# Scaling the second pair of probabilities on ScalarE in the last four steps of a decoder layer

## The chip, the cores and the metric

One core of one Trainium2 chip. The time is device microseconds of one execution of the program; the median of 3 runs before the change is 962.37 us (961.47 to 962.55). Engines are called as in the profile: PE is TensorE, DVE is VectorE, ACT is ScalarE, POOL is GpSimd, SP is SyncE, which issues the DMAs.

## The reference

A decoder layer in float32: x (8 rows of 128 tokens, 512 features) goes through a causal self-attention, then a cross-attention, then a linear layer with 4-bit weights, each with a layer norm in front and a residual behind. The cross-attention, where the change lies, has 8 key heads with 4 query heads each, head size 128, and 256 keys (128 of the context, 128 of the row itself):

```
q, k = rms_norm(latents @ Wq), rms_norm(kv @ Wk);  v = kv @ Wv
probs = softmax(q @ k.T / sqrt(128))     # 32 heads, 128 x 256 each
x = x + (probs @ v) @ Wo
x = x + layernorm(x) @ dequantized_weights.T + bias
```

## The kernel before

The program is two parts, one after the other: self-attention, then `cross_attention_and_linear`. The second part runs 64 steps, s = 8 j + b, for key head j and row b. Each step treats the 4 query heads of one key head for one row. Every float32 operand of a matrix product is split into a high and a low part (`_hi`, `_lo`), and a product is three matmuls. The high part is a Copy on ACT, the low part a subtraction on DVE or POOL.

The order of each engine is written out by hand, and semaphores join the engines. For a step s the work goes like this:

- PE makes scores(s) into two PSUM banks, `ps_s[0]` for heads 0 and 1, `ps_s[1]` for heads 2 and 3. It then does the values of step s-2, the keys and values of s+3, the queries of s+3 and the output projection of s-2.
- DVE takes the row maxima of each bank (`biases`, L1220), ACT the exponentials with their sums (`exps`, L1120), in place in PSUM.
- `probs(s, h)` on DVE (L1227 to L1236) takes for each pair h of heads the reciprocals of the sums (`inv`), multiplies the bank by them into `p` (L1232), and writes the 32x32-block transposes into `p_blocks` (L1236).
- SP stores `p_blocks` to `p_scratch` and loads it back in transposed order into `pT_raw`; one step later ACT makes its high part (`probs_high`, L1143) and POOL its low part (`probs_low`, L1039).
- The keys and queries of the next step come back from memory in the same way; ACT makes their high parts (`queries_keys_high`, L1147 and L1149), DVE the keys' low part (`keys_low`, L1259), POOL the queries' low part (`queries_low`, L1032).
- The output of step s-2 is split by ACT (`output_high`, L1154) and DVE (`output_low`, L1270), projected by PE and added to x by DVE (`residual`, L1266).

In the last round (j = 7, `LAST`) the rows become final one by one, and the linear layer begins between the steps: POOL prepares its weights (`linear_weights`, L1052) and, per row, `row_rstd` and `row_and_bias` (L1068, tile `base`, named `raw_wq` in the trace since it lies in that buffer). DVE takes `statistics`, `normalised` (L1305) and the finished row (`out_row`, L1320), ACT `xn_high` (L1165), DVE `xn_low_row` (L1310), PE the transposes and `linear`.

What matters here is the order on three engines in the last four steps (b = 4 to 7, s = 60 to 63):

- ACT: `exps(s, 0)`, then for b >= 5 `output_high(s-2)` and `exps(s, 1)`, for b = 4 the other way round; `queries_keys_high(s+1)` (not in s = 63); `linear_high(1)` in s = 60; `xn_high(b-4)`; in s = 60 `keys_values(63)`; `probs_high(s-1)`.
- POOL: `row_rstd(b-3)`, ..., `queries_low(s+1)`, `probs_low(s-1)`, and then `linear_weights(4)` (s = 60) or `row_and_bias(b-5)`.
- DVE: `biases(s)`, `normalised(b-4)`, `probs(s, 0)`, then `output_low(s-2)` and `probs(s, 1)` (b = 4: the other way round), `keys_low(s+1)`, `xn_low_row(b-4)`, ..., `residual(s-2)`, `statistics(b-2)`, and `out_row(b-5)`, which stands ahead of the next step's `biases`.

Of the kernel before, what the change touches and what calls it, by code (L numbers as in the profile page):

```python
# [17 lines left out]
ACT = mybir.ActivationFunctionType  # L18
# [13 lines left out]
KV = 2 * S  # L32
# [5 lines left out]
def wait(eng, sem, count):  # L38

    if not (isinstance(count, int) and count <= 0):  # L40
        eng.wait_ge(sem, count)
# [788 lines left out]
def cross_attention_and_linear(nc, mem, io):  # L830
# [7 lines left out]
    with ExitStack() as ctx:  # L838
# [12 lines left out]
        NKV, STEPS, R = 2 * XD, XKVH * B, 32  # L851
        LAST = XKVH - 1
# [15 lines left out]
        total, inv = sb("total", [P, XG]), sb("inv", [P, XG])  # L868
        p = sb("p", [P, XG, KV])
        p_blocks = sb("p_blocks", [P, 8, XG, R])  # L870
# [5 lines left out]
        packed, scale = raw_wq[:, 0:2, :].bitcast(I32), raw_wq[:, 2:4, :]  # L876
# [233 lines left out]
        @block.scalar  # L1110
        def _(act):
            def weights_high(w, raw, landed, count, hi):
                act.wait_ge(landed, 16 * count)
                act.activation(w[0][:], raw[:], ACT.Copy).then_inc(hi, 1)

            def exps(s, h):
                act.wait_ge(bias_ok, 2 * s + h + 1)
                for g in range(2 * h, 2 * h + 2):
                    scores = ps_s[g // 2][:, g % 2 * KV:(g % 2 + 1) * KV]
                    e = act.activation(scores, scores, ACT.Exp, bias=bias[:, g:g + 1],  # L1120
                                       scale=q_rms[:, s % 4, g:g + 1], accum_out=total[:, g:g + 1])
                e.then_inc(exp_done, 1)

            def keys_values(s):

                act.wait_ge(kv_ps, s + 1)
                for t in range(2):
                    i = act.activation(k_squares[:, t, :], kv_rows[:, t, 0:XD], ACT.Square, scale=XD ** -0.5,
                                       accum_out=k_mean[:, t:t + 1])
                i.then_inc(k_mean_ok, 1)  # L1130
                act.activation(v[s % 5][0][:], kv_rows[:, :, XD:], ACT.Copy).then_inc(v_hi, 1)

            def query_sums(s):
                act.wait_ge(q_blocked, s + 1)
                wait(act, q_ms, s)
                for g in range(XG):
                    i = act.activation(q_squares[:, g, :], ps_q[:, g * XD:(g + 1) * XD], ACT.Square, scale=XD ** -0.5,  # L1137
                                       accum_out=q_mean[:, g:g + 1])
                i.then_inc(q_mean_ok, 1)

            def probs_high(s):
                act.wait_ge(p_loaded[s % 4], landed(s))
                act.activation(pT_hi_sb[:], f32(pT_raw[s % 2][:]), ACT.Copy).then_inc(pT_hi, 1)  # L1143

            def queries_keys_high(s):
                act.wait_ge(qk_loaded[s % 4], landed(s))
                act.activation(kT[0][:].rearrange("p (i t c) -> p i t c", i=4, t=2), qk_raw[s % 2][:, :, XG:, :], ACT.Copy,  # L1147
                               scale=key_scale[:, 0:1]).then_inc(kT_hi, 1)
                act.activation(qT[0][:].rearrange("p g (i c) -> p g i c", i=4),  # L1149
                               qk_raw[s % 2][:, :, 0:XG, :].rearrange("p i g c -> p g i c"), ACT.Copy).then_inc(qT_hi, 1)  # L1150

            def output_high(s):
                act.wait_ge(o_ps, s + 1)
                act.activation(oT[0][:].rearrange("p g (i c) -> p g i c", i=4),  # L1154
                               ps_o[:].rearrange("p (i g c) -> p g i c", i=4, g=XG), ACT.Copy).then_inc(o_hi, 1)

            def linear_high(h):
                act.wait_ge(weights_ok, h + 1)
                act.activation(w[0][:, 2 * h:2 * h + 2, :], weights[h], ACT.Copy).then_inc(w_hi, 1)

            def xn_high(b):
                act.wait_ge(xnT_ps, b + 1)
                if b >= 2:
                    act.wait_ge(f_ps, b - 1)
                act.activation(xnT[b % 2][0], ps_xn[:].rearrange("p (c s) -> p c s", c=C), ACT.Copy).then_inc(xn_hi, 1)  # L1165

            keys_values(0)
            query_sums(0)
            keys_values(1)
            query_sums(1)  # L1170
            queries_keys_high(0)
            keys_values(2)
            query_sums(2)
            for s in range(STEPS):
                j, b = divmod(s, B)
                if j < LAST and b == 0:
                    weights_high(wkv[(j + 1) % 2], raw_wkv, wkv_in, j + 1, wkv_hi)
                if b == 2:
                    wait(act, y_ps, B * j)
                    weights_high(wo, raw_wo, wo_in, j + 1, wo_hi)  # L1180
                if j < LAST and b == 3:
                    weights_high(wq[(j + 1) % 2], raw_wq, wq_in, j + 1, wq_hi)
                exps(s, 0)
                if j == LAST and b >= 5:
                    output_high(s - 2)
                    exps(s, 1)
                else:
                    exps(s, 1)
                    if s >= 2:
                        output_high(s - 2)  # L1190
                if s + 1 < STEPS:
                    queries_keys_high(s + 1)
                if j == LAST:
                    if b in (2, 4):
                        linear_high(b // 2 - 1)
                    if b >= 4:
                        xn_high(b - 4)
                if s + 3 < STEPS:
                    keys_values(s + 3)
                if s:  # L1200
                    probs_high(s - 1)
                if s + 3 < STEPS:
                    query_sums(s + 3)
            output_high(STEPS - 2)
            xn_high(4)
            probs_high(STEPS - 1)
            output_high(STEPS - 1)
            xn_high(5)
            xn_high(6)
            xn_high(7)  # L1210

        @block.vector
        def _(dve):
# [10 lines left out]
                        i = dve.tensor_scalar(bias[:, g:g + 1], neg_max[:, g:g + 1], q_rms[:, s % 4, g:g + 1], None, ALU.mult)  # L1224
                    i.then_inc(bias_ok, 1)

            def probs(s, h):  # L1227
                two = slice(2 * h, 2 * h + 2)
                dve.wait_ge(exp_done, 2 * s + h + 1)
                dve.reciprocal(inv[:, two], total[:, two]).then_inc(inv_ok, 1)  # L1230
                dve.wait_ge(inv_ok, 2 * s + h + 1)
                dve.tensor_tensor(p[:, two, :], ps_s[h][:].rearrange("p (g k) -> p g k", g=2),  # L1232
                                  inv[:, two].unsqueeze(2).broadcast_to([P, 2, KV]), ALU.mult).then_inc(p_ok, 1)
                wait(dve, p_stored, 16 * s)
                dve.wait_ge(p_ok, 2 * s + h + 1)
                dve.transpose(p_blocks[:, :, two, :], p[:, two, :].rearrange("p g (m r) -> p m g r", r=R)).then_inc(p_blocked, 1)  # L1236
# [20 lines left out]
            def keys_low(s):  # L1257
                dve.wait_ge(kT_hi, s + 1)
                dve.scalar_tensor_tensor(kT[1][:].rearrange("p (i t c) -> p i t c", i=4, t=2), qk_raw[s % 2][:, :, XG:, :],  # L1259
                                         key_scale[:, 0:1], f32(kT[0][:]).rearrange("p (i t c) -> p i t c", i=4, t=2),  # L1260
                                         ALU.mult, ALU.subtract).then_inc(kT_lo, 1)
# [66 lines left out]
            for s in range(STEPS):  # L1328
                j, b = divmod(s, B)
                biases(s)  # L1330
                if j == LAST:
                    linear_bits(b)
                    if b >= 4:
                        normalised(b - 4)
                probs(s, 0)
                if j == LAST and b >= 5:
                    output_low(s - 2)
                    probs(s, 1)
                else:
                    probs(s, 1)  # L1340
                    if s >= 2:
                        output_low(s - 2)
                if s + 1 < STEPS:
                    keys_low(s + 1)
                if j == LAST and b >= 4:
                    xn_low_row(b - 4)
                if s + 3 < STEPS:
                    values_low(s + 3)
                    queries_blocked(s + 3)
                    keys_blocked(s + 3)  # L1350
                if s >= 2:
                    residual(s - 2)
                if j == LAST:
                    if b >= 2:
                        statistics(b - 2)
                    if b >= 5:
                        out_row(b - 5)
# [219 lines left out]
```

## Time and profile before

| | |
|---|---|
| median of 3 runs | 962.37 us (961.47 to 962.55) |
| profiled execution, its own time | 963.0 us |
| its span, first to last instruction | 961.2 us |
| PE busy | 920.2 us (96%) |
| DVE busy | 727.1 us (76%) |
| ACT busy | 607.3 us (63%) |
| POOL busy | 561.3 us (58%) |
| mean granted TensorE clock | 0.989 |

A busy share is over the whole span. The last four steps and the tail behind them lie from 888 us on. The start of a step is best seen in the first `neg_max` instruction (L1220) of the step on DVE: 888.89, 900.35, 912.10 and 922.96 us for s = 60 to 63.

### The profile page before, as it was taken

The page shows a single profiled execution, that of the slowest core. Times are in us where ns is not written, and L with a number is a line of the kernel's source. Part 1 is how long each engine was busy: PE and PEld are TensorE (multiplying, and loading weights), DVE is VectorE, ACT ScalarE, POOL GpSimd, SP SyncE. Part 2 cuts the span into 40 slices and gives each one's busy share as a digit, 9 for nine tenths or more (in the row PEclk, how much of TensorE's full clock was granted, in tenths as well). Part 3 has the DMA queues.
Part 4 walks back from the last instruction along what each step waited for, and adds up shares of the span by engine and source line. Part 5 has one row for each costly group of instructions (what it writes and reads, how often), then busy time and mean ns, then how long its engine had stood idle before and what let it go on. Part 6 is the DMA issues. An engine that isn't in the chain of part 4 may idle for free.

```text
span 961.2 us, 17529 instructions
## 1 busy us (share of the span) xinstructions
PE 920.2 (96%) x5488; PEld 792.0 (82%) x5496; DVE 727.1 (76%) x1556; ACT 607.3 (63%) x2229; POOL 561.3 (58%) x591
## 2 busy tenths in 40 slices
PE   6899998888999999999999999999999999999987
PEld 5677776677888888888888888888888888888776
DVE  6788888638777777777777777777777777788985
ACT  4688888537656766575666666656766676565541
POOL 6332233338845865686558557855765686558742
PEclk9899999989999999999999999999999999999999
DMA  5000020037665566566656655765566556654431
GB/s 209 12 13 12 13 88 13 1 115 268 223 218 168 175 199 203 173 189 210 214 163 198 213 168 173 228 213 173 168 213 197 165 172 208 209 173 149 156 124 56
DMA packets 101164, 149.84 MB, mean 156 GB/s; under 512 B 11856, under 2 KB 77392, under 8 KB 98896
## 3 DMA queue, kind: packets, MB, share of 16 engines
q1 hardware_dynamic: 101072, 148.71, 48.6%
q8 instruction: 45, 0.74, 0.3%
q14 instruction: 47, 0.39, 0.1%
HBM read 87.85 MB, written 60.82 MB: 155 GB/s over the span
## 4 chain that ended last, share of the span: by engine, by line
PE 72%; DVE 4%; ACT 2%; POOL 2%; issue 1%; DVEq 0%; POOLq 0%
PE ps_kv L73 18%; PE ps_q L73 17%; PE ps_y L73 17%; PE ps_s L73 9%; PE ps_o L73 9%; ACT ps_s L1120 1%; POOL pT_raw L1039 1%; PE ps_f L73 1%; DVE neg_max L1220 0%; DVE p L1232 0%; DVE p_blocks L1236 0%; DVE kT_lo L1259 0%; DVE f_stats L1295 0%; DVE x L1266 0%; POOL qT_lo L1032 0%
## 5 line engine op out<-in xcount | busy, mean ns | idle before, releaser
L1120 ACT ACTIVATE ps_s<-ps_s,bias,q_rms 128x256 f32<-128x256 f32 x256 | 136.7, 535 | 139.8 <-DVE bias L1224 139.8
L1032 POOL TENSOR_TENSOR qT_lo<-qk_raw,qT_hi 128x512 fp32r<-128x512 f32 x64 | 84.5, 1320 | 202.9 <-ACT qT_hi L1149 202.9
L1039 POOL TENSOR_TENSOR pT_raw<-pT_raw,pT_hi_sb 128x1024 fp32r<-128x1024 f32 x63 | 151.7, 2409 | 5.8 <-ACT pT_hi_sb L1143 5.5
L1137 ACT ACTIVATE q_squares<-ps_q 128x128 bf16<-128x128 f32 x256 | 67.2, 277 | 112.5 <-DVE qk_blocks L1254 112.5
L73 PE MATMUL ps_y<-wo_hi,oT_hi 128*128 128x512 f32 x252 | 100.0, 397 | 4.0 <-DVE oT_lo L1270 4.0
L73 PE MATMUL ps_q<-wq_lo,xT_hi 128*128 128x512 f32 x256 | 101.5, 397 | 0.0
L1236 DVE STREAM_TRANSPOSE p_blocks<-p 128x512 f32<-128x512 f32 x128 | 91.1, 712 | 13.3
L73 PE MATMUL ps_q<-wq_hi,xT_hi 128*128 128x512 f32 x256 | 101.1, 395 | 0.0
L73 PE MATMUL ps_q<-wq_hi,xT_lo 128*128 128x512 f32 x256 | 101.1, 395 | 0.0
L73 PE MATMUL ps_y<-wo_lo,oT_hi 128*128 128x512 f32 x252 | 99.5, 395 | 0.0
L73 PE MATMUL ps_y<-wo_hi,oT_lo 128*128 128x512 f32 x252 | 99.4, 394 | 0.0
L1266 DVE TENSOR_TENSOR x<-ps_y,x 128x512 f32<-128x512 f32 x64 | 44.2, 691 | 68.2 <-PE ps_y L73 67.3
L1232 DVE TENSOR_TENSOR p<-ps_s,inv 128x512 f32<-128x512 f32 x128 | 88.5, 691 | 4.4
L1220 DVE TENSOR_REDUCE neg_max<-ps_s 128x2 f32<-128x512 f32 x128 | 87.7, 686 | 5.3
L1254 DVE STREAM_TRANSPOSE qk_blocks<-ps_q 128x512 f32<-128x512 f32 x64 | 45.8, 715 | 42.7 <-PE ps_q L73 42.6
L73 PE MATMUL ps_kv<-wkv_hi,cT_hi 128*128 128x256 f32 x256 | 73.1, 285 | 4.1 <-DVE k_sb L1244 4.1
L73 PE MATMUL ps_s<-kT_hi,qT_hi 128*128 128x256 f32 x256 | 72.6, 284 | 2.7 <-DVE kT_lo L1259 1.3
L73 PE MATMUL ps_kv<-wkv_hi,xT_hi 128*128 128x256 f32 x256 | 72.9, 285 | 0.0
L73 PE MATMUL ps_kv<-wkv_hi,cT_lo 128*128 128x256 f32 x256 | 72.7, 284 | 0.0
L73 PE MATMUL ps_kv<-wkv_hi,xT_lo 128*128 128x256 f32 x256 | 72.6, 284 | 0.0
L73 PE MATMUL ps_kv<-wkv_lo,xT_hi 128*128 128x256 f32 x256 | 72.6, 284 | 0.0
L73 PE MATMUL ps_kv<-wkv_lo,cT_hi 128*128 128x256 f32 x256 | 72.6, 284 | 0.0
(233 smaller groups left out, 2913.3 us busy)
## 6 DMA issues: line engine op xcount, KB each, us to landing
p_scratch<-p_blocks SPq DMA_DIRECT2D x64, 512.0 KB, 3.0
pT_raw<-p_scratch SPq DMA_DIRECT2D x256, 128.0 KB, 3.0
qk_scratch<-qk_blocks SPq DMA_DIRECT2D x64, 384.0 KB, 3.5
qk_raw<-qk_scratch SPq DMA_DIRECT2D x256, 96.0 KB, 3.0
raw_wq<-in_x_wq SPq DMA_DIRECT2D x8, 1024.0 KB, 7.7
raw_wo<-in_x_wo SPq DMA_DIRECT2D x8, 1024.0 KB, 8.2
raw_wkv<-in_x_wkv SPq DMA_DIRECT2D x8, 512.0 KB, 5.0
ctx_raw<-in_ctxT SPq DMA_DIRECT2D x8, 256.0 KB, 2.6
```

Of the source, the lines that this page charges most:

```text
L73: mm = pe.matmul(out, lhsT, rhs, start=start and i == 0, stop=stop and i == len(terms) - 1)
L1032: pool.tensor_tensor(qT[1][:].rearrange("p g (i c) -> p g i c", i=4), qk_raw[s % 2][:, :, 0:XG, :].rearrange("p i g c -> p g i c"), f32(qT ...
L1039: pool.tensor_tensor(raw, f32(raw), f32(pT_hi_sb[:].rearrange("p i t x -> p (i t x)")), ALU.subtract).then_inc(pT_lo, 1)
L1120: e = act.activation(scores, scores, ACT.Exp, bias=bias[:, g:g + 1], scale=q_rms[:, s % 4, g:g + 1], accum_out=total[:, g:g + 1])
L1137: i = act.activation(q_squares[:, g, :], ps_q[:, g * XD:(g + 1) * XD], ACT.Square, scale=XD ** -0.5, accum_out=q_mean[:, g:g + 1])
L1220: dve.tensor_reduce(neg_max[:, two], ps_s[h][:].rearrange("p (g k) -> p g k", g=2), AX.X, ALU.max, negate=True).then_inc(max_ok, 1)
L1232: dve.tensor_tensor(p[:, two, :], ps_s[h][:].rearrange("p (g k) -> p g k", g=2), inv[:, two].unsqueeze(2).broadcast_to([P, 2, KV]), ALU.mu ...
L1236: dve.transpose(p_blocks[:, :, two, :], p[:, two, :].rearrange("p g (m r) -> p m g r", r=R)).then_inc(p_blocked, 1)
L1254: dve.transpose(qk_blocks[:, :, 0:XG, :].rearrange("p j x c -> p x j c"), ps_q[:].rearrange("p (g j r) -> p g j r", g=XG, r=R)).then_inc(q ...
L1266: dve.tensor_tensor(acc[:, b, :], ps_y[:], acc[:, b, :], ALU.add).then_inc(acc_ok, 1)
```

## The change

In steps 60 to 63 DVE no longer multiplies the second pair of heads. DVE takes only the reciprocals of the sums (`inverse_totals`), and ACT makes two Copies of 128x256 with the reciprocal as scale (`second_probs`), one for each head, behind the next step's `queries_keys_high` and ahead of `xn_high` and `probs_high`. The block transposes of the second pair stay on DVE, but behind `output_low` and `keys_low`. On ACT `output_high(s-2)` now stands ahead of `exps(s, 1)` in s = 60 too.

```
+            def second_probs(s):
+                act.wait_ge(inv_ok, 2 * s + 2)
+                for g in (2, 3):
+                    i = act.activation(p[:, g, :], ps_s[1][:, g % 2 * KV:(g % 2 + 1) * KV], ACT.Copy, scale=inv[:, g:g + 1])
+                i.then_inc(p_ok, 1)
...
                 exps(s, 0)
-                if j == LAST and b >= 5:
+                if j == LAST and b >= 4:
                     output_high(s - 2)
                     exps(s, 1)
+                    if s + 1 < STEPS:
+                        queries_keys_high(s + 1)
+                    second_probs(s)
...
-            def probs(s, h):
+            def inverse_totals(s, h):
                 two = slice(2 * h, 2 * h + 2)
                 dve.wait_ge(exp_done, 2 * s + h + 1)
                 dve.reciprocal(inv[:, two], total[:, two]).then_inc(inv_ok, 1)
+
+            def second_probs_blocked(s):
+                wait(dve, p_stored, 16 * s)
+                dve.wait_ge(p_ok, 2 * s + 2)
+                dve.transpose(p_blocks[:, :, 2:, :], p[:, 2:, :].rearrange("p g (m r) -> p m g r", r=R)).then_inc(p_blocked, 1)
...
                 probs(s, 0)
-                if j == LAST and b >= 5:
+                if j == LAST and b >= 4:
+                    inverse_totals(s, 1)
                     output_low(s - 2)
-                    probs(s, 1)
+                    if s + 1 < STEPS:
+                        keys_low(s + 1)
+                    second_probs_blocked(s)
...
-                if s + 1 < STEPS:
+                if s + 1 < STEPS and not (j == LAST and b >= 4):
                     keys_low(s + 1)
```

## Rows read from the trace of the kernel before

**Rows 1.** Chain that ended last, step 60 to tail: start us, us, what.
```profile
895.96 2.81 PE ps_y L73 x12
...
907.01 2.41 DVE kT_lo L1259
...
917.37 0.96 ACT pT_hi_sb L1143
...
918.39 2.61 POOL pT_raw L1039
...
921.00 1.26 POOL raw_wq L1068
...
930.79 1.66 PE ps_o L73 x6
...
945.04 0.95 PE ps_y L84 x4
```

**Rows 2.** Timeline of ACT, steps 60 to 63: start us, length us, instruction.
```profile
895.47 0.42 ACT L1131 ACTIVATE v_hi<-ps_kv 128x256 fp32r<-128x256 f32 x1
...
895.73 1.10 ACT L1143 ACTIVATE pT_hi_sb<-pT_raw 128x1024 fp32r<-128x1024 f32 x1
...
904.08 0.53 ACT L1147 ACTIVATE kT_hi<-qk_raw,key_scale 128x256 fp32r<-128x256 f32 x1
...
904.48 0.65 ACT L1149 ACTIVATE qT_hi<-qk_raw 128x512 fp32r<-128x512 f32 x1
...
905.13 0.60 ACT L1165 ACTIVATE wkv_hi<-ps_xn 128x512 fp32r<-128x512 f32 x1
...
926.70 0.61 ACT L1165 ACTIVATE wkv_hi<-ps_xn 128x512 fp32r<-128x512 f32 x1
```

**Rows 3.** Timeline of POOL, steps 60 to 63; brackets: idle before, releaser.
```profile
896.91 2.40 POOL L1039 TENSOR_TENSOR pT_raw<-pT_raw,pT_hi_sb 128x1024 fp32r<-128x1024 f32 x1
...
900.53 2.40 POOL L1052 TENSOR_TENSOR wq_lo<-raw_wq,wq_hi 128x1024 fp32r<-128x1024 f32 x1
...
905.21 1.29 POOL L1032 TENSOR_TENSOR qT_lo<-qk_raw,qT_hi 128x512 fp32r<-128x512 f32 x1 [1.26 <-ACT qT_hi L1149]
...
906.76 2.38 POOL L1039 TENSOR_TENSOR pT_raw<-pT_raw,pT_hi_sb 128x1024 fp32r<-128x1024 f32 x1 [0.26 <-ACT pT_hi_sb L1143]
...
909.10 1.48 POOL L1068 TENSOR_TENSOR raw_wq<-x,f_bias 128x512 f32<-128x512 f32 x1
...
928.33 2.40 POOL L1039 TENSOR_TENSOR pT_raw<-pT_raw,pT_hi_sb 128x1024 fp32r<-128x1024 f32 x1 [5.25 <-ACT pT_hi_sb L1143]
```

**Rows 4.** Timeline of DVE, steps 61 to 63; brackets: idle before, releaser.
```profile
902.28 0.93 DVE L1305 TENSOR_SCALAR raw_wkv<-x,f_moments,f_rstd 128x512 f32<-128x512 f32 x1
...
905.33 0.14 DVE L1230 RECIPROCAL inv<-total 128x2 f32<-128x2 f32 x1
...
906.94 2.48 DVE L1259 SCALAR_TENSOR_TENSOR kT_lo<-qk_raw,key_scale,kT_hi 128x256 fp32r<-128x256 f32 x1
...
909.95 0.67 DVE L1266 TENSOR_TENSOR x<-ps_y,x 128x512 f32<-128x512 f32 x1
...
911.49 0.69 DVE L1320 TENSOR_TENSOR raw_wq<-ps_f,raw_wq 128x512 f32<-128x512 f32 x1
...
912.10 0.68 DVE L1220 TENSOR_REDUCE neg_max<-ps_s 128x2 f32<-128x512 f32 x1
...
922.35 0.69 DVE L1320 TENSOR_TENSOR raw_wq<-ps_q,raw_wq 128x512 f32<-128x512 f32 x1 [0.80 <-POOL raw_wq L1068]
...
926.33 0.71 DVE L1236 STREAM_TRANSPOSE p_blocks<-p 128x512 f32<-128x512 f32 x1
...
926.97 0.65 DVE L1270 TENSOR_TENSOR oT_lo<-ps_o,oT_hi 128x512 fp32r<-128x512 f32 x1
```

**Rows 5.** Timeline of PE, step 61: output projection of step 59.
```profile
905.46 0.50 PE L73 MATMUL ps_y<-wo_hi,oT_hi 128*128 128x512 f32 x1 [0.36 <-DVE oT_lo L1270]
```

**Rows 6.** Timeline of SP's DMA issues, step 60: query and key loads.
```profile
895.45 2.22 SPq L941 DMA_DIRECT2D qk_raw<-qk_scratch  x4
```

More of the change, by code:

```diff
@@ L1230, in probs @@
                 dve.reciprocal(inv[:, two], total[:, two]).then_inc(inv_ok, 1)
+            def second_probs_blocked(s):
+                wait(dve, p_stored, 16 * s)
+                dve.wait_ge(p_ok, 2 * s + 2)
+                dve.transpose(p_blocks[:, :, 2:, :], p[:, 2:, :].rearrange("p g (m r) -> p m g r", r=R)).then_inc(p_blocked, 1)
+            def probs(s, h):
+                two = slice(2 * h, 2 * h + 2)
+                inverse_totals(s, h)
                 dve.wait_ge(inv_ok, 2 * s + h + 1)
@@ L1342, in _ @@
                         output_low(s - 2)
-                if s + 1 < STEPS:
+                if s + 1 < STEPS and not (j == LAST and b >= 4):
                     keys_low(s + 1)
```

## The prediction, made before the changed kernel ran

> **What bounds the kernel now.** The page first: over the whole span PE is busy 96%, so in the 60 steps that the change leaves alone PE sets the pace. The last four steps are another regime, so I read them by the chain that ended last. The reader is to see that it leaves PE after the output projection of step 60 [rows 1], passes through DVE's low part of the keys in step 61 (2.41 us of its 2.48), and in step 62 through ACT's high part of the probabilities (917.37), POOL's low part (918.39) and POOL's base row (921.00). In step 63 it takes the same way and comes back to PE at 930.79, with the values of step 62. From there to 945.99 it is PE piece on piece. So the multiplication on DVE that the change takes away lies on no late stretch of this chain, while ACT, which gets the new work, does. Three timelines give the slack. DVE's out row of step 62 sat idle 0.80 us until POOL's base row at 922.35 [rows 4]. POOL's last low part of a full step sat idle 5.25 us for ACT's high part [rows 3] and ended at 930.73; the values on PE started 0.06 us later. On the stretch ACT, POOL, base row, out row there is no slack in step 62, and on ACT, POOL, values none in step 63.
>
> **The change part by part.** The price that the trace doesn't show is c, the time by which one of ACT's new Copies (128x256, PSUM to SBUF, scale from a tile) puts off the next instruction. The nearest rows [rows 2]: `v_hi`, PSUM to SBUF with a constant scale, puts the next off by 0.26 (895.47 to 895.73); `kT_hi`, with a scale from a tile but out of SBUF, by 0.40 (904.08 to 904.48); and if nothing overlapped, its whole 0.53. Reading PSUM is cheaper than SBUF by some 0.05 (a 512-wide Copy lasts 0.60 at 905.13 and 0.65 at 904.48), so I take c = 0.40 - 0.04 = 0.36, with 0.26 and 0.53 as ends. Two Copies are 0.72 us a step.
>
> The Trainium skill, "ScalarE: Activation LUTs", section "What ACT_TABLE_LOAD costs", gives an ACTIVATE as 186 ns plus 0.833 ns per element, 93 ns more for each operand taken from a tile, and 93 ns of overlap: an estimate of 0.40 for c, so 0.3 us more on the sum below. The same page, section "Rules for kernel authors", puts multiplications on VectorE rather than ScalarE, which speaks against this change; no row here shows the product on ScalarE.
>
> *Step 60.* ACT's Copies stand ahead of the linear layer's weights, `xn_high`, the keys of step 63 and `probs_high(59)`; `output_high(58)` only trades places with `exps(60, 1)`. The high part of step 59 moves from 895.73 to 896.45, POOL's low part from 896.91 to 897.6, since it began 0.08 after it [rows 2, 3]. What follows on POOL is nearly back to back, so the linear weights' low part moves by 0.67, from 900.53 to 901.2, and ends at 903.6 and no longer at 902.93. DVE's `normalised(1)`, issued at 902.28, ended at 903.21, 0.28 after that POOL instruction [rows 4]; `kT_lo` in step 61 shows the same, 909.42 against POOL's 909.14 [rows 3, 4]. Such a DVE instruction beside POOL ends 0.28 after it. So it now ends at 903.88, and all behind it on DVE is +0.67. The late transposes (+0.9 us) put off SP's store of the probabilities and, queued behind it, the loads of step 62's queries and keys, from 895.45 to 896.4 [rows 6]. With 2.2 us of issue and 3.0 to land (the page) they land at 901.6 and are wanted at 904.08 [rows 2]: nothing. Term: +0.67 at the front of step 61.
>
> *Step 61.* DVE loses the product and takes the output's low part behind a reciprocal that now stands ahead of it (0.14 long, at 905.33, with its gap 0.17 [rows 4]). The projection's start goes from 905.46 [rows 5] to 906.3. `keys_low` comes at 906.2, while POOL's `qT_lo` runs (905.21 to 906.50 [rows 3]), so by the 0.28 above it ends at 906.8, not at 909.42: the 2.48 us stall is gone. The scores of step 62 are then held by the projection (906.3 + 2.81, the length of one in rows 1), and the residual, at 909.95 [rows 4], comes at 909.3; from it to the out row it was 1.54 us, which gives 910.8 instead of 911.49. But what is late next is POOL's base row. ACT's Copies wait for the reciprocal, now at 905.42 to 905.56, and run from 905.6; queued behind the wait are `xn_high` (905.13 before, 906.3 now) and `probs_high`, 0.5 later. It puts POOL's low part from 906.76 to about 907.95, the base row from 909.10 to 910.3, and its end, at 1.29 us (it lasted 1.48 beside `kT_lo`; POOL's other 512-wide instruction lasts 1.29 [rows 3]), to 911.6. The out row starts at 911.65, 0.16 later than before. So the gain of 2.6 us on `kT_lo` is spent: +0.67 comes in, +0.15 goes out. The first maximum of step 62 moves from 912.10 to 912.25 [rows 4].
>
> *Step 62.* ACT's queue is exponentials, output, exponentials, keys, queries, Copies, `xn_high`, `probs_high`. The reciprocal is early enough; +0.72 on the high part that stands on the chain at 917.37. POOL's low part lasted 2.61 beside `kT_lo` against 2.38 in step 61; now `kT_lo` is done before it, so 0.2 comes back. Base row, out row and the maxima of step 63 follow: +0.5. DVE waits for the Copies with its transposes some 0.4 us; behind it stand `xn_low_row` and the residual, which are due later than the base row lets them go.
>
> *Step 63.* No keys and queries here to cover the reciprocal. It stands behind the first pair's transposes, which hold DVE from 926.33 to 926.97 [rows 4], and ends at about 927.12; `xn_high`, at 926.70 before [rows 2], now waits for it 0.45 us and for the Copies 0.72. That is +1.17 for `probs_high(62)`, POOL's low part and the values at 930.79. DVE's last transposes come 0.15 later in the step than before; the store and load of step 63's probabilities are wanted only after the values, linear(3), a transpose and a projection on PE, which have themselves moved by more: nothing.
>
> *Tail.* From 930.79 to 945.99 nothing on the chain waits [rows 1], so what reaches the values reaches the end.
>
> Sum: 0.15 + 0.5 + 1.17 = +1.8 us. The profiled execution took 963.0 us (span 961.2, and 1.8 around it); its sum is 964.8. It lay 0.6 above the median, so for a median I say 962.4 + 1.8 = **964.2 us**. Each 0.01 us in c counts eight times (two Copies, four steps): at c = 0.26 the sum is +1.0 (963.4), at 0.53 it is +3.2 (965.6).
>
> **The rivals.**
>
> *Dear Copies.* If a Copy puts the next off by 0.47 or more, towards its whole length, the sum is +2.7 to +3.2: about 965.3. For it: DVE reads PSUM at the same time, and no row shows a Copy of just this kind. Against it: both neighbouring rows overlap.
>
> *The early keys' low part carries (the other side).* The place is the end of step 61. By the times above the out row starts at 910.9 + 2c there, if the base row holds it, and at 910.8 if that does not. Against 911.49 the place gains from c = 0.29 down, up to 0.7 us. If the Copies also fill time in which ACT would have stood idle, so that steps 62 and 63 add nothing, the whole gains: 962.4 - 0.7 = 961.7. For it: ACT stands idle for long stretches here, `v_hi`'s 0.26 is under that point, and the stall of 2.48 is the largest single thing in these steps. Against it: ACT's idle time lies behind `probs_high`, not ahead of it, and what POOL waited for in step 63 was ACT [rows 3].
>
> *The linear weights do not pass it on.* If step 60's +0.67 does not reach step 61 (POOL catches up, or `normalised(1)` gets in before the weights), the base row of step 61 ends at 910.9 and the sum is 1.8 - 0.67 = +1.1: 963.5. Against it: POOL's row at 900.53 runs across 902.28 even when it starts 0.67 later.
>
> **How the numbers follow.** My forecast (c between 0.26 and 0.46, all terms) has 0.66, its own range 963.4 to 965.0. Dear Copies 0.13, no passing on 0.13, the other side 0.08. The range reaches from 962.6, between the other side and no passing on, to 965.6, the dear end. About 0.2% (1.9 us) is what a measurement of this kernel can tell from no change. Slower by more means above 964.3: all of dear Copies and somewhat under half of my forecast, 0.13 + 0.29 = 0.42. Faster by more means below 960.4, which even the other side's 961.7 does not reach unless step 62 gains too: 0.04. The rest, 0.54, is within 0.2%.
>
> **What would show it.** Right: a Copy at 0.36 to the next start; the linear weights' low part ending about 903.6 and `normalised(1)` 0.28 after it; `kT_lo` of step 61 under 1 us and starting near 906.2; the out rows of steps 61 and 62 both waiting for POOL's base row; first maxima at about 912.25 and 923.6 for steps 62 and 63; the values of step 62 at 932.6, and from there the same tail. Wrong: an out row that waits for PE or for nothing, POOL's low parts not moving with the Copies, or a tail that shrinks.

## The result, and the profile after

The changed kernel takes 964.87 us (median of 15 runs, 962.79 to 967.47) against 962.63 us before (15 runs): ratio 1.0025, 95% interval 1.0016 to 1.0035, so slower by 1.5 to 3.4 us. The forecast was 964.2 us, slower by 1.8.

The profiled execution of the changed kernel took 963.52 us, and its span is 961.4 us, hardly more than 961.2 before. That is no contradiction: single executions differ by some us in their first part (the last section), and here the first row maximum of step 60 comes at 887.28 us against 888.89. What the change touches begins there. So I measure from that instruction to the start of the last out row; the rows of the changed kernel on DVE:

```profile
887.28 0.67 DVE L1229 TENSOR_REDUCE neg_max<-ps_s 128x2 f32<-128x512 f32 x1
...
898.74 0.67 DVE L1229 TENSOR_REDUCE neg_max<-ps_s 128x2 f32<-128x512 f32 x1
...
910.74 0.68 DVE L1229 TENSOR_REDUCE neg_max<-ps_s 128x2 f32<-128x512 f32 x1
...
922.11 0.68 DVE L1229 TENSOR_REDUCE neg_max<-ps_s 128x2 f32<-128x512 f32 x1
...
958.21 0.69 DVE L1338 TENSOR_TENSOR raw_wq<-ps_q,raw_wq 128x512 f32<-128x512 f32 x1 [1.78 <-PE ps_q L84]
```

The stretch is 70.93 us; before it was 958.04 - 888.89 = 69.15. So +1.78 us, beside a forecast of +1.8. The stretch does not hold all of the difference of the medians, 2.24 us. An execution's own time is longer than its span by 1.72 to 1.85 us in all executions of the kernel before whose span is on record, and by 2.08 to 2.17 in all 15 of the changed kernel (and in the two other kernels below that have the change in all four steps). These 0.35 us lie outside the first and last instruction, and no run shows where they come from. In the table each column is the time since the first row maximum of step 60: the first maximum of steps 61, 62 and 63, the first matmul of the values of step 62, and the start of the last out row.

| kernel | step 61 | step 62 | step 63 | values 62 | last out row |
|---|---|---|---|---|---|
| before | 11.46 | 23.21 | 34.07 | 41.90 | 69.15 |
| changed | 11.46 | 23.46 | 34.83 | 43.78 | 70.93 |
| difference | 0 | +0.25 | +0.76 | +1.88 | +1.78 |

Where it went is in the chain that ended last (columns: start us, us, what), which answers to [rows 1]:

```profile
906.38 2.40 POOL pT_raw L1039
908.77 1.27 POOL raw_wq L1068
...
915.40 0.85 ACT p L1160 x2
916.25 0.49 ACT wkv_hi L1171
916.74 0.96 ACT pT_hi_sb L1143
917.70 0.07 issue
917.76 2.39 POOL pT_raw L1039
920.15 1.25 POOL raw_wq L1068
...
926.65 0.47 ACT p L1160
927.12 0.49 ACT wkv_hi L1171
927.61 0.96 ACT pT_hi_sb L1143
928.57 0.07 issue
928.63 2.38 POOL pT_raw L1039
931.01 0.04 issue
931.06 1.65 PE ps_o L73 x6
```

The stalled `kT_lo` that stood on the chain before is gone from it. ACT's two new Copies (`p`, L1160) are on it instead, in steps 62 and 63, each time with `xn_high`, `probs_high`, POOL's low part and its base row (or PE's values) behind them. In step 61 the chain now runs through POOL, whose low part at 906.38 sat idle 1.51 us for ACT's high part; that part stood behind the Copies at 904.02 (both rows are in the section on the prediction).

### The profile page after: what moved, and what is told of

The parts are those of the page before. It is cut to its first block, busy times and chain, and to the rows that moved or that the text cites. A ratio compares the mean times of both kernels' runs of the same rounds, so it can differ in the third digit from the quotient of the medians.

```text
span 961.4 us, 17533 instructions
## 1 busy us (share of the span) xinstructions
PE 918.6 (96%) x5488; PEld 791.2 (82%) x5496; DVE 723.4 (75%) x1552; ACT 610.9 (64%) x2237; POOL 559.8 (58%) x591
## 4 chain that ended last, share of the span: by engine, by line
PE 71%; DVE 3%; POOL 2%; ACT 2%; issue 1%; DVEq 0%; POOLq 0%
PE ps_kv L73 18%; PE ps_y L73 17%; PE ps_q L73 17%; PE ps_o L73 9%; PE ps_s L73 9%; POOL pT_raw L1039 1%; ACT ps_s L1120 1%; PE ps_f L73 1%; DVE neg_max L1229 0%; POOL qT_lo L1032 0%; DVE p L1250 0%; DVE p_blocks L1254 0%; POOL raw_wq L1068 0%; DVE raw_wq L1303 0%; ACT q_squares L1137 0%
## 5 line engine op out<-in xcount | busy, mean ns | idle before, releaser
L1254 DVE STREAM_TRANSPOSE p_blocks<-p 128x512 f32<-128x512 f32 x124 | 88.2, 711 | 12.9
L1250 DVE TENSOR_TENSOR p<-ps_s,inv 128x512 f32<-128x512 f32 x124 | 85.7, 691 | 4.2
```

## The experiments

Each is read by the stretch above, in one profiled execution of each kernel, since a few tenths of a us are lost in the spread of whole executions. Ten of them were also timed over several executions, and for these a ratio to the kernel before is given; step 60 alone and step 63 alone ran once.

The stretch ends at the start of the last out row, so it leaves out the last store. At the very end SP waits for that store (columns: us in total, times, longest), in the kernel before and in step 61 alone:

```profile
SPq L1007 <- DMA out<-raw_wq: 1.7, 1, 1.7
...
SPq L1007 <- DMA out<-raw_wq: 2.8, 1, 2.8
```

The wait is 2.8 to 2.9 us in all five kernels below that make the change in one step only, and 1.7 us in all others, the changed kernel included. Why is not shown. So in those five some 1.1 us come on top of what the stretch says; their ratios contain them.

**The change in step 61 alone** (step 60, 62 and 63 as before).

```
-                if j == LAST and b >= 4:          # changed kernel, on ACT and on DVE
+                if j == LAST and b == 5:
...
+                elif j == LAST and b >= 5:        # the order of the kernel before
```

> The change in step 61 alone; steps 60, 62 and 63 as before. I measure the stretch from the first row maximum of step 60 to the start of the last out row in the profile: 69.15 us before, 70.93 with the whole change. My theory: each step's two Copies (0.72 us) cost only where they stand ahead of work that POOL and PE wait for, and step 61 alone also removes the 2.4 us stall of the keys' low part. Without step 60's delay the base row of step 61 then ends about 0.5 us earlier than before, so the stretch is 68.5 to 68.8 (-0.35 to -0.65) and the kernel is slightly faster. Rival, the Copies cost their 0.72 us in every step whatever else moves, so each step is worth a quarter of the whole: +0.45, 69.6.

Measured: 68.75 us (-0.40); step 62 begins at 22.85, 0.36 earlier. Ratio 1.0005 (0.9990 to 1.0019). So the Copies do not cost their 0.72 us wherever they are made: in this step the stretch gains. The kernel as a whole does not. From step 60's first row maximum to the end of the span it takes 73.08 us against 72.31 before, because of the last store.

**The change in steps 61 to 63.**

```
-                if j == LAST and b >= 4:
+                if j == LAST and b >= 5:
```

> The change in steps 61 to 63, step 60 as before. My theory: step 60 costs 0.6 to 0.7 us through ACT's queue, POOL's low part of the linear weights and the row normalisation on VectorE that ends with it; so the stretch from step 60's first row maximum to the last out row is 70.1 to 70.35 (whole change 70.93, before 69.15). Rival, step 60's delay is hidden by the base row on POOL that holds step 61 anyway: 70.8 to 71.0, no change from the whole.

Measured: step 62 at 22.83, 0.63 ahead of the whole change; the stretch is 70.56, not 70.1 to 70.35. Ratio 1.0016 (1.0000 to 1.0031). Step 62 lasted 11.57 us against 11.37 in the whole change, and in it the granted clock fell (columns: window, its length, busy time of PE, PEld, DVE, ACT and POOL, clock, DMA share, GB/s):

```profile
910.00:915.00 5.00, 4.95 (x24) 3.85 (x23) 4.00 (x12) 1.77 (x6) 2.21 (x4) 1.00 0.82 240
915.00:920.00 5.00, 3.50 (x12) 2.65 (x11) 3.44 (x7) 4.09 (x10) 2.22 (x2) 0.72 0.16 63
```

Up to step 62 the theory holds, and the end is 0.2 outside its numbers. The slower clock accounts for that. From the start of PE's output projection to the residual that waits for it on DVE the changed kernel took 3.10 us (915.52 to 918.62), this one 4.65:

```profile
916.92 0.58 PE L73 MATMUL ps_y<-wo_hi,oT_hi 128*128 128x512 f32 x1 [1.50 <-DVE oT_lo L1291]
...
921.50 1.30 POOL L1068 TENSOR_TENSOR raw_wq<-x,f_bias 128x512 f32<-128x512 f32 x1
...
921.57 0.69 DVE L1287 TENSOR_TENSOR x<-ps_y,x 128x512 f32<-128x512 f32 x1 [2.52 <-PE ps_y L73]
...
923.12 0.67 DVE L1341 TENSOR_TENSOR raw_wq<-ps_q,raw_wq 128x512 f32<-128x512 f32 x1
```

So the out row came 0.32 us after the end of POOL's base row, which it follows by 0.09 to 0.11 us in the changed kernel: an estimate of 0.2 us for the clock.

**Step 60 alone** (the first experiment's edit with another step).

```
-                if j == LAST and b >= 4:
+                if j == LAST and b == 4:
```

> The change in step 60 alone, steps 61 to 63 as before; one look, read by the stretch from step 60's first row maximum to the last out row (69.15 us before, 70.93 with the whole change). My theory: the two Copies reach the end through GpSimd's low part of the linear weights, beside which the row normalisation of step 61 ends: step 61 starts as before, step 62 0.6 to 0.75 later, and the stretch is 69.7 to 69.9. Rival, PE sets step 60's end and the base row hides the rest: 69.1 to 69.3.

Measured: step 61 at 11.47, step 62 at 23.94 (+0.73), the stretch 69.88 (+0.73). POOL's low part of the linear weights and DVE's normalisation beside it, of this kernel:

```profile
899.12 2.39 POOL L1052 TENSOR_TENSOR wq_lo<-raw_wq,wq_hi 128x1024 fp32r<-128x1024 f32 x1
```

```profile
900.15 1.64 DVE L1326 TENSOR_SCALAR raw_wkv<-x,f_moments,f_rstd 128x512 f32<-128x512 f32 x1
```

The normalisation ends at 901.79, 0.28 after POOL, and lasts 1.64 instead of 0.93 [rows 4].

**Step 63 alone.**

```
-                if j == LAST and b >= 4:
+                if j == LAST and b == 7:
```

> The change in step 63 alone; one look, read by the same stretch. My theory: 0.4 us of waiting for the reciprocal behind the first pair's transposes and 0.72 for the two Copies stand ahead of the last high part that GpSimd and then the values on PE wait for: the values of step 62 start 1.05 to 1.2 later than before against step 60's first row maximum (41.90), and the stretch is 70.1 to 70.4. Rival, a part of it is taken back by the shorter work of VectorE or in PE's tail: 69.2 to 69.8.

Measured: the values of step 62 at 43.06 (+1.16), the stretch 70.21 (+1.06). By the table and these runs, alone or in the whole, the steps are worth +0.73, -0.4, +0.5 and +1.1.

**Copies made twice.**

```
                 for g in (2, 3):
+                    act.activation(q_squares[:, 2 * g - 4:2 * g - 2, :].rearrange("p a b -> p (a b)"),
+                                   ps_s[1][:, g % 2 * KV:(g % 2 + 1) * KV], ACT.Copy, scale=inv[:, g:g + 1])
+                for g in (2, 3):
                     i = act.activation(p[:, g, :], ...
```

> The whole change, with each of ScalarE's two Copies of a step made twice (the first time into a tile that nothing reads). My theory, ScalarE's queue ahead of the high part of the probabilities sets the end in steps 60 to 63: 0.72 us more in each of four steps, and nothing to hide it, so the stretch from step 60's first row maximum to the last out row grows by 2.7 to 3.0 us, to 73.6 to 74.0. Rival, the cost of the change lies in VectorE's new order (transposes behind the keys' low part) and in its waits, not in ScalarE's queue: VectorE then waits 0.72 longer for the probabilities, in two of the steps only, 71.0 to 72.0.

Measured: 75.43 us; ratio 1.0055 (1.0034 to 1.0075). The values of step 62 start at 46.66, that is 2.88 later than with single Copies, as 4 x 0.72 says. The tail behind them lasted 28.77 us against 27.15, and there the clock fell, after PE had waited 1.47 us at 931.00 and 1.83 us at 935.89:

```profile
930.00:935.00 5.00, 3.06 (x12) 2.18 (x12) 3.10 (x7) 3.10 (x7) 1.52 (x1) 1.00 0.25 105
935.00:940.00 5.00, 4.11 (x12) 3.24 (x13) 2.54 (x5) 0.60 (x1) 4.09 (x5) 0.69 0.52 157
940.00:945.00 5.00, 5.00 (x24) 4.14 (x23) 1.98 (x3) 1.55 (x2) 0.00 (x0) 0.97 0.00 0
```

So the expectation held up to the values and missed the tail, which I had taken as rigid. The clock fell in step 62 of this run too (0.68 from 920 to 925 us); there it did not set the time, since the out row still sat idle 0.44 us for POOL's base row.

**Copies behind `probs_high`, steps 61 to 63.**

```
-                if j == LAST and b >= 4:
+                if j == LAST and b >= 5:
...
                         queries_keys_high(s + 1)
-                    second_probs(s)
...
                 if s:
                     probs_high(s - 1)
+                if j == LAST and b >= 5:
+                    second_probs(s)
```

> The change in steps 61 to 63 with ScalarE's two Copies moved behind the high part of the step before's probabilities; step 60 as before. The same two Copies, only their place in ScalarE's queue differs from the run of steps 61 to 63 (stretch from step 60's first row maximum to the last out row: 70.56 us; before 69.15). My theory, what costs is the place ahead of the high part that GpSimd waits for: 68.3 to 68.8, faster than before, for the early keys' low part then costs nothing on ScalarE; the later transposes may hold the next load of probabilities by a few tenths. Rival, the Copies cost wherever they stand, since VectorE waits for them with its transposes and holds what is behind: 70.0 to 71.0.

Measured: 68.28 us (-0.87), against 70.56 with the same Copies ahead. Ratio 0.9993 (0.9978 to 1.0008). DVE does wait for them with its transposes, longest in step 62:

```profile
908.39 0.83 ACT L1160 ACTIVATE p<-ps_s,inv 128x256 f32<-128x256 f32 x2
```

```profile
909.32 0.71 DVE L1248 STREAM_TRANSPOSE p_blocks<-p 128x512 f32<-128x512 f32 x1 [0.78 <-ACT p L1160]
...
919.99 0.71 DVE L1248 STREAM_TRANSPOSE p_blocks<-p 128x512 f32<-128x512 f32 x1 [1.94 <-ACT p L1160]
```

In steps 61 and 62 these waits cost nothing: the out rows behind them still sat idle 0.17 and 0.19 us for POOL's base row. The tail is 27.46 us against 27.25 before; whether the later transposes cause this is not shown. This is the clearest of the runs: same work, same engine, 2.3 us apart by its place in the queue (some 0.2 of it is the clock's fall in the other run).

**Base row ahead, on the whole change.** POOL makes the base rows of steps 61 and 62 ahead of `queries_low`, in time in which it was idle.

```
+                if j == LAST and b in (5, 6):
+                    row_and_bias(b - 5)
                 if s + 1 < STEPS:
                     queries_low(s + 1)
...
-                    if b >= 5:
+                    if b >= 7:
                         row_and_bias(b - 5)
```

> The whole change, with GpSimd's base row moved ahead of the queries' low part in steps 61 and 62, into time in which GpSimd was idle. The base row then no longer waits for ScalarE's Copies. My theory, the out row of VectorE, which waits for the base row, hands the Copies' time on to the next step's row maxima: without that, steps 61 and 62 lose it and only step 60's and step 63's price stays. The stretch from step 60's first row maximum to the last out row falls from 70.93 to 68.5 to 69.0 (before 69.15). Rival, the Copies cost through the values on PE or through VectorE's waits: 70.5 to 71.0.

Measured: 68.86 us, 2.07 under the changed kernel. Ratio 1.0005 (0.9992 to 1.0018). DVE's out row of step 61 now follows the statistics without idle time:

```profile
909.48 0.69 DVE L1286 TENSOR_TENSOR x<-ps_y,x 128x512 f32<-128x512 f32 x1 [0.69 <-PE ps_y L73]
...
910.93 0.18 DVE L1317 BATCH_NORM_AGGREGATE f_moments<-f_stats 128x2 f32<-128x6 f32 x1
911.04 0.69 DVE L1340 TENSOR_TENSOR raw_wq<-ps_f,raw_wq 128x512 f32<-128x512 f32 x1
```

So the base row was what took the early keys' gain back in step 61 and passed the Copies on in step 62. The change still does not pay with this order on POOL: the next run, without the change, has a stretch 0.41 us shorter.

**Base row ahead, on the kernel before.**

The same edit on the kernel before:

```
+                if j == LAST and b in (5, 6):
+                    row_and_bias(b - 5)
                 if s + 1 < STEPS:
                     queries_low(s + 1)
...
-                    if b >= 5:
+                    if b >= 7:
                         row_and_bias(b - 5)
```

> The kernel before, with GpSimd's base row moved ahead of the queries' low part in steps 61 and 62; nothing of the change. My theory, the out row of step 62 sat idle 0.80 us for the base row and nothing else was as late, while in step 61 the stall of the keys' low part holds VectorE anyway: the third step starts 0.7 to 1.1 us earlier, the stretch from step 60's first row maximum to the last out row is 68.2 to 68.6 (before 69.15). Rival, the projection or the row's statistics are due at the same moment: 69.0 to 69.2.

Measured: 68.45 us (-0.70); step 62 as before (23.24, the stall of `kT_lo` is still there), step 63 0.87 earlier. Ratio 0.9977 (0.9961 to 0.9994).

**VectorE's new order alone.** The kernel before with `keys_low` ahead of the second pair in steps 61 and 62, the product on DVE.

```
                     output_low(s - 2)
+                    if s + 1 < STEPS:
+                        keys_low(s + 1)
                     probs(s, 1)
...
-                if s + 1 < STEPS:
+                if s + 1 < STEPS and not (j == LAST and b >= 5):
                     keys_low(s + 1)
```

> VectorE's new order alone, without ScalarE's Copies: the kernel before, with the next keys' low part moved ahead of the second pair's reciprocal, product and transposes in steps 61 and 62. ScalarE's queue is as before. My theory: the stall of the keys' low part behind GpSimd's low part of the probabilities (2.48 us in step 61) goes, since it now stands beside the queries' low part or nothing, and nothing is paid on ScalarE: the stretch from step 60's first row maximum to the last out row is 67.7 to 68.2 (before 69.15), the kernel faster by about 1.0 to 1.4 us. Rival, the stall was slack (the base row of GpSimd holds the out row anyway) or the second pair's product, now later, holds the next scores: 69.0 to 69.6.

Measured: 68.46 us (-0.69), ratio 0.9985 (0.9969 to 1.0001). Step 62 begins 0.99 earlier, as expected, but step 63 only 0.66: in step 62 `probs_high` waited for the load of step 61's probabilities, whose transposes were now later.

```profile
914.81 1.07 ACT L1143 ACTIVATE pT_hi_sb<-pT_raw 128x1024 fp32r<-128x1024 f32 x1 [0.42 <-DMA pT_raw<-p_scratch]
```

The stretch fell between the numbers of the theory and those of the rival: I had left this load out of the expectation.

**What pays, put together.** Step 61's part of the change with the base rows ahead, both edits as above:

```
+                if j == LAST and b in (5, 6):     # POOL, ahead of queries_low
+                    row_and_bias(b - 5)
...
+                if j == LAST and b == 5:          # ACT and DVE, the change in one step
```

> The change in step 61 alone, with GpSimd's base row ahead of the queries' low part in steps 61 and 62: the part of the change that pays, without the wait that gave the gain back. My theory: step 62 starts 1.1 to 1.4 us earlier than before, step 63 another 0.7 to 1.1, and the stretch from step 60's first row maximum to the last out row is 67.0 to 67.5 (before 69.15), the kernel faster by 1.6 to 2.1 us, about 0.2%. Rival, the load of step 61's probabilities or the projection on PE is next and keeps half of it: 68.0 to 68.5.

Measured: 67.09 us (-2.06); step 62 1.32 earlier, step 63 2.21. Ratio 0.9988 (0.9971 to 1.0005).

The same, with `probs_high` ahead of `xn_high` in step 63:

```
-                    if b >= 4:
+                    if 4 <= b < 7:
                         xn_high(b - 4)
...
                     probs_high(s - 1)
+                if j == LAST and b == 7:
+                    xn_high(b - 4)
```

> The change in step 61 alone, with the base rows ahead (stretch 67.09), and in step 63 ScalarE's high part of the probabilities ahead of the high part of the normalised row. My theory, the values of step 62 on PE wait in step 63 for just this high part: they start up to 0.49 earlier, until PE itself is not free, and the stretch is 66.5 to 66.9. Rival, PE is not free earlier, since the projection before the values ends at the same moment: 67.0 to 67.2.

Measured: 66.90 us (-2.25), ratio 0.9990 (0.9977 to 1.0003). The values start at 39.47 instead of 39.85, and PE no longer waits for POOL ahead of them (0.20 us in the run before this). The tail grew by 0.19 us, so half of the 0.38 was left.

And without any Copy on ScalarE, the base rows ahead and `keys_low` moved on DVE only:

```
+                    if b == 5:
+                        keys_low(s + 1)
                     output_low(s - 2)
+                    if b == 6:
+                        keys_low(s + 1)
                     probs(s, 1)
...
-                if s + 1 < STEPS:
+                if s + 1 < STEPS and not (j == LAST and b >= 5):
                     keys_low(s + 1)
```

> No Copies on ScalarE: the kernel before with GpSimd's base row ahead of the queries' low part in steps 61 and 62, and the keys' low part on VectorE ahead of the output's low part in step 61 and behind it, ahead of the second pair's product, in step 62. It asks whether the early keys' low part needs ScalarE's help at all. My theory: not much; the stall goes, the projection starts some 0.3 later than with the Copies in step 61 alone, and the stretch is 67.1 to 67.6 (67.09 with them, 69.15 before). Rival, the product left on VectorE holds the next scores or the next load of probabilities: 68.0 to 68.6.

Measured: 67.61 us (-1.54), just above the expected numbers; ratio 0.9991 (0.9979 to 1.0003). The stretch of step 61's part is 0.52 us shorter, but that is not ScalarE's help alone, for the two kernels also differ in DVE's order, and it does not reach the end. All three have shorter stretches than both kernels. Counted to the end of the span, the last store included, they take 71.43, 71.27 and 70.79 us in the order given, against 71.61 for the base rows alone and 72.31 before. So the one without any Copy on ScalarE is the shortest, and that the Copies pay is not shown. By whole executions the intervals of all three hold 1, and only the kernel before with the base rows ahead is timed as faster beyond its interval. A part of that is the mix of its executions: six of its ten, but 8 of 35 of the kernel before, had a mean clock of 0.991 to 0.993, and among these the medians are 0.65 us apart (960.07 and 960.72), as its stretch says. Which of the four is best is not settled by the times.

## Why the prediction was right

**The price of a Copy.** I took c = 0.36 us. ACT's rows of the changed kernel:

```profile
891.94 0.85 ACT L1160 ACTIVATE p<-ps_s,inv 128x256 f32<-128x256 f32 x2
892.66 1.08 ACT L1165 ACTIVATE wq_hi<-raw_wq 128x1024 fp32r<-128x1024 f32 x1
...
904.02 0.84 ACT L1160 ACTIVATE p<-ps_s,inv 128x256 f32<-128x256 f32 x2 [0.51 <-DVE inv L1239]
904.75 0.60 ACT L1171 ACTIVATE wkv_hi<-ps_xn 128x512 fp32r<-128x512 f32 x1
...
926.27 0.84 ACT L1160 ACTIVATE p<-ps_s,inv 128x256 f32<-128x256 f32 x2 [0.30 <-DVE inv L1239]
927.00 0.60 ACT L1171 ACTIVATE wkv_hi<-ps_xn 128x512 fp32r<-128x512 f32 x1
```

Two Copies put the next instruction off by 0.72 to 0.73: c = 0.36. Dear Copies are out. The estimate by the Trainium skill, "ScalarE: Activation LUTs", section "What ACT_TABLE_LOAD costs", was 0.40; the measurement decides.

**Step 60**, forecast +0.67: measured +0.73, through the very instructions named. The weights' low part on POOL ends at 902.05, and `normalised(1)` 0.28 later:

```profile
899.67 2.38 POOL L1052 TENSOR_TENSOR wq_lo<-raw_wq,wq_hi 128x1024 fp32r<-128x1024 f32 x1
...
906.38 2.40 POOL L1039 TENSOR_TENSOR pT_raw<-pT_raw,pT_hi_sb 128x1024 fp32r<-128x1024 f32 x1 [1.51 <-ACT pT_hi_sb L1143]
908.74 1.30 POOL L1068 TENSOR_TENSOR raw_wq<-x,f_bias 128x512 f32<-128x512 f32 x1
```

```profile
900.66 1.67 DVE L1323 TENSOR_SCALAR raw_wkv<-x,f_moments,f_rstd 128x512 f32<-128x512 f32 x1
...
903.87 0.12 DVE L1239 RECIPROCAL inv<-total 128x2 f32<-128x2 f32 x1
903.91 0.66 DVE L1288 TENSOR_TENSOR oT_lo<-ps_o,oT_hi 128x512 fp32r<-128x512 f32 x1
904.50 0.64 DVE L1277 SCALAR_TENSOR_TENSOR kT_lo<-qk_raw,key_scale,kT_hi 128x256 fp32r<-128x256 f32 x1
...
910.13 0.69 DVE L1338 TENSOR_TENSOR raw_wq<-ps_f,raw_wq 128x512 f32<-128x512 f32 x1 [0.76 <-POOL raw_wq L1068]
...
921.50 0.69 DVE L1338 TENSOR_TENSOR raw_wq<-ps_q,raw_wq 128x512 f32<-128x512 f32 x1 [1.25 <-POOL raw_wq L1068]
```

That this delay does not pass on is out, by step 60 alone.

**Step 61**, forecast +0.15 at the start of step 62: measured +0.25. `kT_lo` lasts 0.64 instead of 2.48, where and when forecast, and the out row at 910.13 sits idle 0.76 us for the base row. The term I sized wrongly on the way is the reciprocal: I let it put the output's low part off by 0.17, the gap to the product in [rows 4], which reads the reciprocal. The output's low part does not read it and started 0.04 after it (903.87 to 903.91). It is not on the path here.

**Step 62**, forecast +0.5: measured 0.76 - 0.25 = +0.51. The out row now idles 1.25 us for the base row, 0.80 before [rows 4].

**Step 63**, forecast +1.17: measured 1.88 - 0.76 = +1.12. ACT sits idle 0.30 for the reciprocal, as the row at 926.27 says, and the two Copies follow. Against the step's first row maximum they start 0.42 later than `xn_high` did before; I had said 0.45.

**Tail**, forecast 0: measured -0.10.

So the mechanism was right in each step. The terms were off by up to 0.1 us with both signs, so that their sum came out within 0.04 is luck.

The other side, the early keys' low part, was a real gain with the wrong neighbour: the base row on POOL holds it, and with the base row out of the way even the stretch of the whole change is 0.29 us under the kernel before. My break-even for it, c = 0.29, counted the Copies of step 61 only. With those of step 60, which reach the same base row, the out row starts at 910.2 + 4c and the break-even is 0.32, still under the 0.36 measured.

The median came out 0.7 above the forecast, 2.2 us over the kernel before instead of 1.8. The stretch gives 1.78, and the interval of the ratio holds that. I had taken the 1.8 us around the span as fixed, without a reason; it grew by 0.35. I gave 0.54 to a change within 0.2% and 0.42 to slower by more. The median (0.25%) lies in the second, the stretch (0.18%) in the first, and the interval does not tell them apart.

## What to carry to other kernels

Work moved to an engine that is idle a third of the time still costs the time for which it holds that engine (0.72 us a step here) if it stands in that engine's order ahead of something that another engine is waiting for. The same two Copies 1.1 to 1.6 us later in the step had no price that the stretch shows (68.28 us, against 68.46 with DVE's new order and no Copies). Price a moved instruction by what is queued behind it, and a removed stall by the next wait of the engine that had it. Where the idle row of a waiting engine names a short instruction that had long been ready (here the base row), moving that one is the cheaper change. And when a stretch stands for the whole kernel, look at what lies behind it too: here the last store took back a part or all of what some of the stretches had gained.

## What the runs showed of the hardware

Executions of one kernel differ by up to 5 us (962.79 to 967.47 here), and much of it lies in the first part, in the granted clock. In the 14 profiled executions step 60 began between 886.75 and 890.70 us, though the program up to there is the same. Four of them had a clock of 0.81 to 0.82 from 20 to 30 us and began it at 886.75 to 887.28; the other ten had 0.50 to 0.68 and began it at 888.62 or later. The window from 20 to 30 us of the changed kernel, whose step 60 began at 887.28:

```profile
20.00:30.00 10.00, 7.38 (x43) 6.58 (x44) 8.33 (x24) 6.25 (x21) 3.32 (x5) 0.81 0.01 2
```

and of the run with the change in step 63 alone, whose step 60 began at 890.70:

```profile
20.00:30.00 10.00, 7.56 (x34) 7.03 (x35) 6.48 (x16) 5.55 (x19) 2.06 (x3) 0.50 0.01 2
```

In the one the clock is for a part of the window at the lower of its two levels (1.2 GHz), in the other throughout. By contrast the step from 60 to 61 lasted 11.45 to 11.49 us in every kernel that left ScalarE's Copies single.

TensorE's clock also fell late, in the two kernels above: after PE had waited 1.50 us (916.92, the change in steps 61 to 63), 1.50 us (918.89, Copies twice) and 1.83 us (935.89, Copies twice). A wait of this length alone does not bring it about. The changed kernel has such waits, and its clock stayed at 1.00 from 905 to 955 us:

```profile
915.52 0.50 PE L73 MATMUL ps_y<-wo_hi,oT_hi 128*128 128x512 f32 x1 [1.51 <-DVE oT_lo L1288]
...
926.88 0.50 PE L73 MATMUL ps_y<-wo_hi,oT_hi 128*128 128x512 f32 x1 [1.50 <-DVE oT_lo L1288]
```

What else it takes is not shown.

The keys' low part (`kT_lo`, two inputs in SBUF) and the row normalisation on VectorE ended 0.28 to 0.29 us after a GpSimd instruction that had begun before them, in each case read here. The Trainium skill, "SBUF — State Buffer", section "Who interferes with whom", says that a VectorE instruction with two inputs in SBUF contends with a GpSimd instruction that reads SBUF. The runs agree: `kT_lo` alone lasts 0.44 to 0.47 us, beside GpSimd up to 2.52 (the kernel before with the base row ahead).
